# A residual chain on one core: half a product ahead of a wait, two L3 tiles side by side, a split ahead of the norm, and moves of 2 KB runs

## What is computed

```python
x = x + L0(x)                      # gated causal scans, a soma product, a layer norm
x = x + (x @ W[cat] + b[cat])      # L1, 512 x 512 per sequence
h = relu(x @ W1[lang] + b1[lang])  # L2, adapter 512 -> 128 -> 512
x = x + layernorm(x + h @ W2[lang] + b2[lang]) * gamma[lang] + beta[lang]
x = x + (x @ weight[subj].T + bias[subj])   # L3, 512 x 512 per sequence
```

## Time and profile before

| | us |
|---|---|
| median of three runs | 729.51 (729.51 to 729.77) |
| the profiled execution | 728.34 |
| its span, first to last instruction | 726.5 |
| PE busy | 717.6 (99%), clock granted in full |
| DVE busy | 542.7 (75%) |
| ACT busy | 372.0 (51%) |
| POOL busy | 121.8 (17%) |

### The profile page before, as it was taken

How to read it: one execution, slowest core, us unless ns; L and a number is a source line. 1 busy time by engine, 2 the same in 40 slices (tenths; PEclk the granted TensorE clock), 3 DMA queues, 4 the chain that set the end, 5 groups by cost and what they waited for, 6 DMA issues and landing times.

```text
span 726.5 us, 10057 instructions
## 1 busy us (share of the span) xinstructions
PE 717.6 (99%) x3285; PEld 591.1 (81%) x3285; DVE 542.7 (75%) x816; ACT 372.0 (51%) x554; POOL 121.8 (17%) x220
## 2 busy tenths in 40 slices
PE   9999999999999999999999999999999999999998
PEld 8877888888888888888888888887878888888886
DVE  5799796695596597587679569886878888677574
ACT  4365446446535635545544633664666565473540
POOL 2000030022013004004004005204322122021110
PEclk9999999999999999999999999999999999999999
DMA  7959307934943962970990871845165745433322
GB/s 205 267 115 180 61 1 109 190 79 86 195 96 58 198 119 41 189 145 6 179 190 1 126 249 33 212 164 203 44 170 164 202 102 190 133 106 96 85 75 88
DMA packets 134959, 93.55 MB, mean 129 GB/s; under 512 B 92255, under 2 KB 119934, under 8 KB 132878
## 3 DMA queue, kind: packets, MB, share of 16 engines
q1 hardware_dynamic: 128366, 86.56, 51.5%
q10 hardware_dynamic: 6368, 6.59, 3.1%
q0 software_dynamic: 192, 0.00, 0.0%
HBM read 32.28 MB, written 25.20 MB: 79 GB/s over the span
## 4 chain that ended last, share of the span: by engine, by line
PE 88%; DVE 7%; issue 1%; ACT 1%; DMA 1%; POOL 1%; SPq 0%; ACTq 0%; DVEq 0%; POOLq 0%
PE pc L705 11%; PE pc L707 11%; PE pc L706 11%; PE pt L705 7%; PE pt L706 7%; PE pt L707 7%; PE pm L705 5%; PE pm L707 5%; PE pm L706 5%; PE pm L823 4%; PE pm L824 4%; PE pm L825 4%; PE pm L712 2%; DMA ctx_t<-xt_scratch 1%; DVE x_l L1764 1%
## 5 line engine op out<-in xcount | busy, mean ns | idle before, releaser
L705 PE MATMUL pc<-x_h,wg_h 128*128 128x512 f32 x224 | 87.6, 391 | 1.7 <-DVE s_l L1771 1.6
L707 PE MATMUL pc<-x_h,wg_l 128*128 128x512 f32 x224 | 87.2, 389 | 0.0
L706 PE MATMUL pc<-x_l,wg_h 128*128 128x512 f32 x224 | 87.2, 389 | 0.0
L1563 DVE TENSOR_TENSOR_SCAN stage_b<-alpha,carry,stage_b 128x512 f32<-128x512 f32 x64 | 78.5, 1268 | 0.0
L705 PEld LDWEIGHTS pc<-x_h,wg_h 128*128 128x128 f32 x224 | 42.0, 188 | 12.4 <-issue 3.9
L1198 ACT ACTIVATE ctx_t<-ctx_t,col_all 128x512 f32<-128x512 f32 x32 | 23.1, 723 | 54.0 <-DVE ctx_t L1543 54.0
L823 PE MATMUL pm<-t_h,wt_h 128*128 128x512 f32 x128 | 50.2, 392 | 0.6 <-DVE t_l L1576 0.5
L825 PE MATMUL pm<-t_h,wt_l 128*128 128x512 f32 x128 | 49.9, 390 | 0.0
L824 PE MATMUL pm<-t_l,wt_h 128*128 128x512 f32 x128 | 49.9, 390 | 0.0
L705 PE MATMUL pm<-wo_h,s_h 128*128 128x512 f32 x128 | 49.8, 389 | 0.0
L706 PE MATMUL pm<-wo_l,s_h 128*128 128x512 f32 x128 | 49.8, 389 | 0.0
(11 more groups left out here) (277 smaller groups left out, 1875.0 us busy)
## 6 DMA issues: line engine op xcount, KB each, us to landing
x_planes<-x_pairs SPq DMA_DIRECT2D x56, 256.0 KB, 7.0
xt_scratch<-x_t SPq DMA_DIRECT2D x8, 1024.0 KB, 9.9
n_scratch<-stage_a SPq DMA_DIRECT2D x8, 1024.0 KB, 9.5
ctx_t<-xt_scratch SPq DMA_DIRECT2D x16, 512.0 KB, 7.1
x_pairs<-n_scratch SPq DMA_DIRECT2D x14, 512.0 KB, 5.8
out_dram<-x_tok SPq DMA_DIRECT2D x28, 256.0 KB, 2.5
mod<-mod_scratch ACTq DMA_DIRECT2D x8, 512.0 KB, 3.7
x_planes<-stage_b SPq DMA_DIRECT2D x60, 64.0 KB, 2.0
```

The lines of the kernel that those rows point to most:

```text
L705: nc.tensor.matmul(acc, ah, bh, start=start and q == 0, stop=False)
L706: nc.tensor.matmul(acc, ah, bl, start=False, stop=False)
L707: last = nc.tensor.matmul(acc, al, bh, start=False, stop=stop and q == n - 1)
L1563: nc.vector.tensor_tensor_scan(tr[:, m % 2, :], alpha[:, 1 + d:2 + d].to_broadcast([P, BLK]), tr[:, m % 2, :], carry[:, D - d, m:m + 1], A ...
```

## The change

Five edits. (1) `l1_product` can run in two halves of six matmuls; the first half of block 1's product 1 is issued ahead of the four `xx_product(0, 0, k)`, the second half where the whole was. (2) L3's tiles 0 and 1 of block 0 are made together (`l3_pair`): each chunk of x3 serves both before the next is waited for. (3) For block 2, ACT's `x2_parts(2, 1)` and DVE's `x2_lo_part(2, 1)` stand ahead of block 1's first normalise and of its first squares and y_sum(3, 0). (4) `normalise` writes the features of blocks 1 to 6 in another order (q before c), so that a square's quarter is one run of 512 elements in stage_b: a move is now 32 runs of 2 KB on both sides, and `scale_n2` reads through the view `moved`. For block 2's step all six of ACT's moves stand ahead of its ReLU (before: three). (5) SP does `load_y(3)` ahead of `store_out(0, 0)`.

```diff
-        squares_q = stage_b[:, :, :].rearrange("p a e -> p (a e)").rearrange("p (c q r) -> p c q r", c=NC, q=4)
+        moved = x_planes[:, :, :].rearrange("p a (c k i) -> p c k a i", c=NC, k=TILES)
...
-            part, tok = slice(32 * a, 32 * a + 32), slice(P * a, P * a + P)
-            engine.dma_start(x_planes[32 * q:32 * q + 32, :, tok], squares_q[part, :, q, :]).then_inc(n2_in, 16)
+            engine.dma_start(x_planes[32 * q:32 * q + 32, a, :], stage_b[32 * a:32 * a + 32, q, :]).then_inc(n2_in, 16)
...
             load_l2(1)
+            load_y(3)
             store_out(0, 0)
-            load_y(3)
             store_out(0, 1)
...
-                wh, wl = l1_w(b)
-                product(l1_bank(i, m)[:, :], of_x(wh, wl, 0, out_cols(m))).then_inc(l1_mm, 1)
+                pairs = of_x(*l1_w(b), 0, out_cols(m))
+                bank = l1_bank(i, m)[:, :]
+                if part == 0:
+                    product(bank, pairs[:2], stop=False)
+                elif part == 1:
+                    product(bank, pairs[2:], start=False).then_inc(l1_mm, 1)
+                else:
+                    product(bank, pairs).then_inc(l1_mm, 1)
...
+            def l3_pair(j):
+
+                wh, wl = l3_w(j // PER_SEQ)
+                ch, cl = x3_parts_of(j)
+                for c in range(NC):
+                    pe.wait_ge(x3_hi, j * NC + c + 1)
+                    pe.wait_ge(x3_lo, j * NC + c + 1)
+                    for k in range(2):
+                        tok = out_cols(k)
+                        last = product(l3_bank(j, k)[:, :], [(ch[:, c, tok], cl[:, c, tok], wh[:, c, :], wl[:, c, :])],
+                                       start=(c == 0), stop=(c == NC - 1))
+                        if c == NC - 1:
+                            last.then_inc(l3_mm, 1)
...
-                for m in range(1, NC):
-                    l1_product(1, 0, m)
+                l1_product(1, 0, 1, 1)
+                l1_product(1, 0, 2)
+                l1_product(1, 0, 3)
                 turn_n2(0)
                 w1_product(1, 0)
...
-                l3_tile(0, 0)
-                l3_tile(0, 1)
+                pe.wait_ge(x3_sum, 2)
+                l3_pair(0)
...
             l1_product(1, 0, 0)
+            l1_product(1, 0, 1, 0)
             for k in range(TILES):
...
-                                     x_planes[:, m, :].rearrange("p (a k i) -> p k a i", k=TILES, a=4), ACT.Identity,
+                                     moved[:, m, :, :, :], ACT.Identity,
...
-                nc.scalar.activation(stage_a[:, k, :], pm[k][:, :], ACT.Identity, bias=nbias[:, k:k + 1],
+                src, dst = pm[k][:, :], stage_a[:, k, :]
+                if not turned_by_pe(j):
+                    src = src.rearrange("p (c q i) -> p q c i", c=NC, q=4)
+                    dst = dst.rearrange("p (q c i) -> p q c i", c=NC, q=4)
+                nc.scalar.activation(dst, src, ACT.Identity, bias=nbias[:, k:k + 1],
...
                     x2_parts(i, 0)
+                    if i == 2:
+                        x2_parts(i, 1)
                     normalise(i - 1, 0)
-                    x2_parts(i, 1)
+                    if i > 2:
+                        x2_parts(i, 1)
...
-                before = {2: 3, LAST: len(BY_ACT)}.get(i, 0)
+                before = 6 if i in (2, LAST) else 0
...
                     x2_lo_part(i, 0)
+                if j == 0:
+                    x2_lo_part(i, 1)
                 turn_squares(i - 1, 0)
                 if more and not turned:
                     y_sum_part(i + 1, 0)
-                if j != 1:
+                if j > 1:
                     x2_lo_part(i, 1)
```

More of the change, by code:

```diff
@@ L914, in turn_y, with l1_product @@
                 turn(pt[c % 2], [n_tile(i, k)[:, out_cols(c)] for k in range(TILES)]).then_inc(ty_done, 1)
-            def l1_product(i, b, m):
+            def l1_product(i, b, m, part=None):
                 if m == 0:
```

## The result

The changed kernel takes **725.97 us** in the median (725.11 to 732.15, 13 runs) where the kernel before, beside it, takes 729.89 (728.51 to 738.61, 13 runs). The ratio is 0.9939, 95% interval 0.9911 to 0.9967. It lies inside the range, but nearest to the number of the short issues (726.2), which did not happen. The ratio is not the quotient of the two medians, which is 0.9946. The profiled execution took 725.11 us (span 723.3), 3.23 less than the one of before.

The account below looks back on a forecast made before the run. PE, busy 717.6 of 726.5 us, was taken as the bound, so only its stops could be won: 0.60 + 0.69 + 1.57 + 0.49 = 3.35 less 1.1 gives 2.25 us. Forecast 727.3 us, range 725.7 to 729.1.

Parts of the forecast that it names:

- short issues: Rival: a move of 32 runs issues in 0.33 to 0.45 us, ReLU 2 comes on time, 726.2 us; chance 0.30.
- Gap A: PE stop at block 0's transposes (497.14 us), 1.47 lost; six matmuls fill it, 0.60 us won net.
- new stop: PE wait for x2_lo(1, 0) ahead of block 1's product 2, 0.68 us, replacing part of the old stop.
- Gap B: PE stop in block 0's L3 tiles, waiting for x3_lo's third chunk; pairing tiles wins the whole 0.69 us.
- Gap C: PE stop ahead of block 2's product 3; goes with x2 ahead of the norm and an earlier load, 1.57 won.
- Gap D: PE stop at block 3's third product, behind n2's sums; goes as the moves start earlier, 0.49 us won.
- The six moves: Six ACT issues ahead of ReLU 2 take 4.2 us; new PE stop at block 2's transposes costs about 1.1 us.
- Other places of the moves: New moves outside block 2's step cost or win nothing; no PE stop stands behind them in blocks 3 to 7.
- crowded issues: Rival: SP's and ACT's issues beside each other take 0.99 us each, PE stands 2.8 us, 729.0 us; chance 0.13.
- slow PSUM pattern: Rival: pieces of 32 double ACT's normalise to 1.57 us, kernel 2.3 us slower, 731.8 us; chance 0.07.
- The sum: Whole change: 3.35 us won, 1.1 given back, 2.25 net; 727.3 us, set 1.17 above the profiled execution's 726.1.

Follow-up runs that it names:

- no_half: Changed kernel with block 1's product 1 whole again behind block 0's transposes; 726.91 us, ratio 0.9931.
- no_pair: Changed kernel with L3 tiles 0 and 1 of block 0 one after the other again; 727.36 us, ratio 0.9922.
- old_a: The kernel before, unchanged, one more profiled execution; 231.31 us from block 0's first transposes to the last matmul's end, where the first execution has 226.15.
- c_only: Kernel before with only block 3's x load ahead of the first store and both x2 pieces of block 2 ahead of the norm; 726.51 us, ratio 0.9931.
- d_only: Kernel before with only all six ACT moves ahead of ReLU 2; 728.72 us, ratio 0.9972.
- ab_d: Kernel before with the half product, L3 tiles 0 and 1 together and all six ACT moves ahead of ReLU 2; 729.50 us, ratio 0.9956.
- acts3_early: Changed kernel with three ACT moves ahead of ReLU 2 and x2_lo(1, 0) ahead of block 0's last two norm2_stats; 725.53 us, ratio 0.9914.
- old_moves: Changed kernel with the moves of before (128 runs of 512 B) and the old order of normalise; 726.52 us, ratio 0.9966 to the kernel before.
- moves_only: Kernel before with only the new moves (32 runs of 2 KB) and their order of normalise and scale_n2; 728.70 us, ratio 0.9966.
- again: The changed kernel, unchanged, run once more beside the kernel before; median 725.86 us, ratio 0.9938, its profiled execution 730.37 us.
- old_b: The kernel before, unchanged, another profiled execution; 732.60 us.
- again2: The changed kernel, unchanged, run a further time beside the kernel before; 726.10 us, ratio 0.9899.
- ab_only: Kernel before with only the half product ahead of block 0's transposes and L3 tiles 0 and 1 together; 737.28 us, ratio 1.0054.
- old_c: The kernel before, unchanged, another profiled execution; 228.38 us from block 0's first transposes to the last matmul's end.

## Why the prediction was right and wrong

- **Gap A** was right: new stop 0.67 for 0.68, and `no_half` lengthens the stretch by 0.61 for 0.60.
- **Gap B** was right: no bracket after, 0.60 lost with `no_pair`.
- **Gap C** was right as a mechanism and is the step that failed in size. "Won: 1.57" took one execution's wait for a transfer (0.57 us) as the kernel's. Four executions waited 0.57 to 2.47 us and lost 1.49 to 3.39 there, and `old_a` lost 1.6 more to the clock. `c_only`, with the edits of that term alone, won 2.6 to 3.0 us; it shuts D too, so this stands against 1.57 + 0.49 = 2.06.
- **Gap D**: the price of 0.49 was again the least of four, and the reason was wrong. It put its closing down to the moves' earlier start, six ahead of the ReLU. That is enough (`d_only`, `ab_d`) but not needed: in `c_only` and `acts3_early` D is shut with three, as soon as C is gone.
- **The six moves** cost 0.81 and 0.08 of restart, 0.89, for 1.1 forecast. In the whole change they give nothing for it: in the trace of `acts3_early` this stop is gone and D stays shut. `ab_d` shows where they are worth 7 to 8 us: with A and B done and C still open. The price of an issue didn't go with its runs: 591 and 612 ns in the median on SP and ACT after, 601 and 628 in the earlier trace rows. Short issues are out as a rival: a quarter of the runs took 2% off. The Trainium skill (Perfetto Trace Analysis, DMA Instruction — HWDGE) says that the generation of the descriptors lies inside the profiled issue. That fewer runs would make it shorter was the prediction's inference, and these rows do not bear it out.
- **Other places of the moves**: "cost or win nothing elsewhere" was low by part of the 0.7 to 0.9 us that `old_moves` and `moves_only` show. "In blocks 3 to 7 no PE stop stands behind them" holds in 14 of 20 traces; in the other six, `again` among them, PE lost 0.39 to 0.76 us behind block 7's moves. The crowded issues, told for block 2, did not come there (six in 4.03 us).
- **The slow PSUM pattern** is out: normalise took 780 ns in the median after and 781 before.
- **The sum**: with the medians of the four executions C and D lose 1.96 + 0.87 = 2.83 instead of 1.90, 0.93 more, and the six moves cost 0.2 less. 2.25 + 0.93 + 0.2 = 3.4 us is what the changed kernel's medians stand below the executions of before under 732 us (729.38). That it fits so well is partly luck: it is an estimate from four traces, and two of them (`old_a`, `old_b`) are of executions over 732. The prediction carried the 1.17 us between the profiled execution and the median over to the changed kernel. The 0.93 would be most of that distance, and the change removes them; that was the mistake in one number. That they are the same is argued: before 497 us the profiled execution was not quicker than others (497.14 against 497.15 and 497.52), so that it must have been behind. (The changed kernel's profiled execution stands 0.86 below its median for another reason: it was quick ahead of 497 us, 496.35 where `again2` has 497.70.) The rest of the 3.9 comes from the third of the executions at 732 us and more, which pull the median of before up.

## What to carry to other kernels

Before costing a stop that ends on a DMA, look at it in several executions: its size in one profile is a draw, and where a profiled execution is quicker than the median, such stops are the first to suspect. Time won ahead of a stop that waits for a transfer is given back at it, and more if the clock falls behind the longer stop and so puts the next small transfers behind large ones: `ab_only` won 1.3 us and came out 4 us slower by the ratio, 7 by the medians. So take the transfer's stop off first, and where small moves are wanted soon, see to it that they are issued ahead of large loads.

## What the runs showed of the hardware

- The granted clock stayed at 0.50 (1.2 GHz) for about three microseconds behind some stops in which PE lost 2.1 to 4.6 us, and that cost 1.4 to 1.8 us each time (`old_a`, `ab_only` twice, `ab_d`, and at 39 us `again` and `old_b`). It did not fall behind 2.00 (`moves_only`), 3.33 (gap D of `old_a`) or 3.39 us (`old_c`).
- A move of 64 KB landed in 2.0 us ahead of two pairs of loads of 512 KB and in up to 9.2 us behind their first.
- The issue of a move from SBUF to SBUF took about 0.6 us with 32 runs as with 128 (medians 591 and 601 ns on SP), and single ones up to 1.4 us where two engines issued side by side (`again`, block 7).
